# Attention keys gathered straight into key order, instead of block gathers followed by copies in SBUF

## The reference, cut to what matters

```
H, G, HD = (8, 4, 32)        # 8 query heads, 4 key/value groups, 32 channels
BLOCK = 16                   # tokens in a cache block
WINDOW = 128                 # a token attends to the 128 keys before it
SCALE = 256.0 ** (-0.5)
NBLK = 257                   # table entries of a batch
k_blocks, v_blocks: (B * NBLK, G, BLOCK, HD)
```

## Time and profile before

| | us |
|---|---|
| three timed runs | 1230.33, 1234.93, 1240.94 (median 1234.93) |
| the profiled execution | 1232.31, of which the span from first to last instruction is 1230.5 |

### The profile page before, as it was taken

One profiled execution on the slowest core, in us unless ns is written; L12 is line 12 of the kernel. 1 busy time (PEld: TensorE's weight loads), 2 busy tenths in 40 slices (PEclk: granted clock), 3 DMA queues, 4 the chain that ended last, 5 costly groups with the idle time before them and its releaser, 6 DMA issues.

```text
span 1230.5 us, 18499 instructions
## 1 busy us (share of the span) xinstructions
PE 957.4 (78%) x5487; PEld 722.4 (59%) x5487; DVE 577.4 (47%) x1672; ACT 371.8 (30%) x1034; POOL 345.6 (28%) x385
## 2 busy tenths in 40 slices
PE   3899889406999983982397878969787688999985
PEld 2677667205777763652275766657544466777774
DVE  5567766122666540584272744628323244444323
ACT  2334234102333320112171634627232223222210
POOL 7000532552555551033412221310003420343100
PEclk9899899757999996985596887969787599999999
DMA  8042207294444427632776554430211120332221
GB/s 321 5 164 42 71 31 270 94 254 135 135 133 132 135 68 170 231 115 59 151 170 110 109 107 94 93 57 0 94 47 39 65 92 9 93 96 86 77 85 52
DMA packets 71577, 132.04 MB, mean 107 GB/s; under 512 B 19841, under 2 KB 54106, under 8 KB 69168
## 3 DMA queue, kind: packets, MB, share of 16 engines
q1 hardware_dynamic: 48399, 75.49, 21.1%
q0 software_dynamic: 20800, 53.52, 16.7%
q10 hardware_dynamic: 2304, 2.13, 0.6%
HBM read 87.39 MB, written 43.30 MB: 106 GB/s over the span
## 4 chain that ended last, share of the span: by engine, by line
PE 29%; DMA 11%; issue 4%; DVE 4%; POOL 3%; ACT 3%; DVEq 0%; POOLq 0%; ACTq 0%
PE ps L436 8%; DMA early<-newblk,new_i 6%; PE ps L648 4%; DMA big<-newblk,new_i 4%; PE ps L666 3%; PE ps L1967 2%; PE ps L2110 1%; PE ps L2066 1%; PE ps L2033 1%; POOL sent_d L732 1%; PE ps L2038 1%; POOL early L970 1%; PE ps L1990 1%; POOL big L970 1%; PE ps L2067 1%
## 5 line engine op out<-in xcount | busy, mean ns | idle before, releaser
L732 POOL DMA_INDIRECT sent_d<-mid,slot_i x96 | 98.0, 1021 | 175.1 <-DVE mid L567 148.3
L723 POOL DMA_INDIRECT back_d<-early,mid x95 | 93.6, 986 | 96.3 <-DVE early L707 61.4
L694 DVE TENSOR_TENSOR early<-early,ps 128x96 f32<-128x96 f32 (+1 forms) x134 | 37.3, 279 | 141.8 <-ACT early L682 98.0
L666 PE MATMUL ps<-early 96*128 (+1 forms) x346 | 98.7, 385 | 0.9 <-DVE early L701 0.9
L677 ACT ACTIVATE early<-ps 128x256 f32<-128x256 f32 x134 | 51.4, 384 | 136.2 <-PE ps L638 126.5
L648 PE MATMUL ps<-big,early 128*128 x380 | 88.4, 357 | 5.0 <-ACT early L677 2.8
L467 DVE TENSOR_TENSOR hidl<-work,hidh 128x512 fp32r<-128x512 f32 (+1 forms) x56 | 38.8, 692 | 104.9 <-ACT hidh L461 98.3
L473 ACT ACTIVATE work<-ps 128x512 f32<-128x512 f32 (+1 forms) x56 | 33.4, 597 | 161.5 <-PE ps L436 141.3
L638 PE MATMUL ps<-late,mid 128*128 128x128 f32 x268 | 52.8, 279 | 30.5 <-DMA mid<-sent_d 30.5
L1967 PE MATMUL ps<-early 128*128 128x176 f32 x256 | 69.1, 376 | 4.5 <-DVE early L1592 4.1
L648 PEld LDWEIGHTS ps<-big,early 128*128 128x128 f32 x380 | 61.6, 195 | 18.7 <-issue 15.8
(11 more groups left out here) (378 smaller groups left out, 2224.7 us busy)
## 6 DMA issues: line engine op xcount, KB each, us to landing
mid<-sent_d SPq DMA_DIRECT2D x134, 130.0 KB
big<-back_d SPq DMA_DIRECT2D x16, 512.0 KB
early<-back_d SPq DMA_DIRECT2D x16, 256.0 KB, 3.3
sent_d<-big SPq DMA_DIRECT2D x26, 130.0 KB
big<-in_gate SPq DMA_DIRECT2D x1, 3072.0 KB, 11.9
big<-in_up SPq DMA_DIRECT2D x1, 3072.0 KB, 18.0
early<-early SPq DMA_DIRECT2D x32, 96.0 KB
big<-big SPq DMA_DIRECT2D x32, 96.0 KB
```

Of the source, the lines that this page charges most:

```text
L666: last = nc.tensor.matmul(ps[:, 6 + j % 2, 0:D], L.hTb[j % 2][0:f1 - f0, h * P:(h + 1) * P], L.down[0:f1 - f0, h, bass.ds(owners[j] * D, D ...
L694: nc.vector.tensor_tensor(L.hb[j % 2], L.sgb[j % 2], ps[:, 2 + j % 2, F:2 * F], ALU.mult)\
L723: nc.gpsimd.indirect_dma_start(out=back_d, out_offset=bass.IndirectOffsetOnAxis(ap=xblk[b % XRING][:, D:D + 1].bitcast(I32), axis=0), in_= ...
L732: nc.gpsimd.indirect_dma_start(out=sent_d, out_offset=bass.IndirectOffsetOnAxis(ap=L.slot_i[:, i:i + 1], axis=0), in_=L.rows[c][:, t, n, : ...
```

## The change

Everything below concerns how keys and values reach `kv2`, and what that needs.

- Cache and `newblk` are viewed as rows of two tokens (2 KB, 8 rows for a block). A batch's 176 keys are 88 such rows, and each is gathered straight to its partition: `old_keys(g)` issues 4 gathers of 88 rows (one for each batch) from the cache, `new_keys(g)` 4 from `newblk`. Partition p of a batch holds keys 2p and 2p+1. The copies of SP (line 866) and of POOL (line 970) are gone, and so are the staging windows.
- `kv2` has 8 slots (`KVRING`) instead of 4, four in `early` and four in `big`. `old_keys(g)` waits for `o_ps` of tile g - 8.
- The columns of the scores come in another order (even keys, then odd), which the constant for the mask takes up. Keys are transposed as 88 + 88 instead of 96 + 80 partitions, and ACT copies the transposed probabilities in one piece of 88x512 instead of two.
- The gathers need one index for each row of two keys: 88 for each batch. `pe_spread` makes them on PE by 8 small matmuls in layer 0 (chunk 3, m = 1) from the block numbers `blkw` and the new-block numbers that DVE's `windows_new` gives; `key_rows` turns them into integers on DVE at m = 2. PE waits for `index` ahead of the 8, and for `spread_used` at m = 3.
- In POOL's program `old_keys` 0 and 1 stand behind the writes of chunk 0, 2 and 3 behind those of chunk 1, 4 and 5 behind those of chunk 2. The memset of `Qbd` stands behind `new_keys` 0 and 1 and ahead of 2 and 3.
- `raw3`, a weight of layer 3 (640 KB), goes to `low0` and is loaded by SP between expert blocks 16 and 17 instead of behind the expert rows; layer 3's shared weights are loaded by SP when the first chunk's batches are done instead of after its first tile's.
- PE's loop over the 4 chunks is written out instead of a hardware loop.

```diff
+HB, HK, KVRING = BLOCK // 2, WK // 2, 8
...
-        kvw = [x[:, 0:ROW].rearrange("p (o n) -> p o n", o=BLOCK) for x in (early, big)]
         halves = [early[:, ROW:2 * ROW], big[:, 8448:8448 + ROW]]
-        kv2 = [x[:, j * (ROW // 2):(j + 1) * (ROW // 2)].rearrange("p (h b n) -> p h b n", h=2, b=BPT)
-               for x in halves for j in range(2)]
+        kv2 = [x[0:HK, j * (ROW // 2):(j + 1) * (ROW // 2)].rearrange("p (b o n) -> p b o n", b=BPT, o=2)
+               for x, n in ((early, 4), (big, 2), (halves[1], 2)) for j in range(n)]
...
             for b in range(NBK):
                 sp_block(sp, L1, b)
+                if b == XRING:
+                    sp.dma_start(raw3, a["raw3"]).then_inc(s["raw3"], 16)
...
-            for g in range(NT):
...
-                for q in range(BPT):
-                    sp.dma_start(kv2[t][0:6 * BLOCK, 0, q, :], kvw[half][p0 + q * WB:p0 + q * WB + 6, :, :])\
-                        .then_inc(s["into%d" % t], 16)
...
+            def old_keys(g):
                 t, c = g % TPC, g // TPC
...
+                if g >= TPC:
+                    pool.wait_ge(s["gold%d" % t], 16 * TPC + LANDED * c)
+                if g >= KVRING:
+                    pool.wait_ge(s["o_ps"], O_CREDIT + BPT * (g - KVRING + 1))
                 for q in range(BPT):
...
+                    gather(kv2[g % KVRING][:, q, :, :].rearrange("p o n -> p (o n)"), cache8,
+                           old_i[:, q * NT + g:q * NT + g + 1], s["gold%d" % t])
+
+            def new_keys(g):
+                t, c = g % TPC, g // TPC
+                pool.wait_ge(s["gold%d" % t], 16 * TPC + LANDED * (c + 1))
+                if g >= TPC:
+                    pool.wait_ge(s["gone%d" % t], landed(t) + LANDED * c)
+                for q in range(BPT):
+                    gather(kv2[g % KVRING][:, q, :, :].rearrange("p o n -> p (o n)"), newblk8,
+                           new_i[:, q * NT + g:q * NT + g + 1], s["gone%d" % t],
+                           bounds_check=SEGS * HB - 1, oob_is_err=False)
+
+            pool.wait_ge(s["spread_used"], 1)
...
                 pool.wait_ge(s["scattered"], (c + 1) * (16 * TPC))
                 if c == 0:
+                    pool.wait_ge(s["turn_ps"], NBK + 2 * TPC)
+                    old_keys(0)
+                    old_keys(1)
+                if c == 1:
                     pool.wait_ge(s["turn_ps"], NBK + NT)
-                    old_rows(2)
-                    old_rows(3)
+                    old_keys(2)
+                    old_keys(3)
+                if c == 2:
+                    old_keys(4)
+                    old_keys(5)
 
             pool.wait_ge(s["scattered"], 16 * NT)
-            for g in range(TPC):
-                new_rows(g)
+            for g in range(2):
+                new_keys(g)
             pool.wait_ge(s["qkv_end"], 1)
             nc.gpsimd.memset(Qbd, 0.0).then_inc(s["qzero"], 1)
+            for g in range(2, TPC):
+                new_keys(g)
             pool.wait_ge(s["qsb_ready"], NCH)
-            pool.wait_ge(s["fint_sb"], 2)
-            for g in range(TPC):
-                turn_rows(g)
-            for g in range(TPC, NT + 2):
+            for g in range(TPC + 2, NT + 2):
                 if g < NT:
...
+                    old_keys(g)
+                new_keys(g - 2)
...
-                nc.scalar.activation(PTs[0:96, n % 2, 0, :], ps[0:96, 4 + n % 2, 0:256], ACT.Copy)
-                nc.scalar.activation(PTs[0:80, n % 2, 1, :], ps[0:80, 4 + n % 2, 256:512], ACT.Copy)\
+                nc.scalar.activation(PTs[0:HK, n % 2, :, :].rearrange("p h n -> p (h n)"), ps[0:HK, 4 + n % 2, :], ACT.Copy)\
...
+            def key_rows():
+                dve.wait_ge(s["spread_ps"], 1)
+                n = BPT * NT
+                for j, idx in enumerate((old_i, new_i)):
+                    last = nc.vector.tensor_scalar(idx[:, :], ps[0:HK, 5, j * n:(j + 1) * n], float(HB),
+                                                   F["pairoff"][0:HK, :], ALU.mult, ALU.add)
+                last.then_inc(s["spread_used"], 1)
...
+            def pe_spread():
+                pe.wait_ge(s["index"], AT_SHIFT)
+                pe.wait_ge(s["slots_ready"], NCH - 2)
+                WR = BPT * WB
+                for j, x in enumerate((blkw, ix[:, 32:48])):
+                    for q in range(BPT):
+                        o = (j * BPT + q) * NT
+                        last = nc.tensor.matmul(ps[0:HK, 5, o:o + NT], F["spread"][0:WR, q * HK:(q + 1) * HK],
+                                                x[0:WR, :], start=True, stop=True)
+                last.then_inc(s["spread_ps"], 1)
...
+                    if tc == 3 and m == 1:
+                        pe_spread()
+                    if tc == 3 and m == 3:
+                        pe.wait_ge(s["spread_used"], 1)
...
                 if q == 0:
...
-                nc.tensor.transpose(ps[:, n % 2, 0:96], kv2[t][0:96, 0, q, 0:KW], ident[0:96, 0:96])
-                nc.tensor.transpose(ps[:, n % 2, 96:WK], kv2[t][0:80, 1, q, 0:KW], ident[0:80, 0:80])\
+                    pe.wait_ge(s["gone%d" % t], landed(t) + LANDED * (tc + 1))
+                nc.tensor.transpose(ps[:, n % 2, 0:HK], rows[:, q, 0, 0:KW], ident[0:HK, 0:HK])
+                nc.tensor.transpose(ps[:, n % 2, HK:WK], rows[:, q, 1, 0:KW], ident[0:HK, 0:HK])\
```

More of the change, by code:

```diff
@@ L749, in build @@
         L1.into0, L1.gone0 = [0] * AHEAD, [0] * ORING
-        L3.into0 = [loaded(j) + NCH * TURNED for j in range(AHEAD)]
-        L3.gone0 = [landed(j) + NCH * NEWROWS for j in range(ORING)]
+        L3.into0 = [loaded(j) for j in range(AHEAD)]
+        L3.gone0 = [landed(j) + NCH * LANDED for j in range(ORING)]
         gu3 = a["gu3"].rearrange("p (g k n) -> p g k n", g=2, k=KD)
@@ L1487, in _ @@
                     if tc == 3 and m == 2:
+                        key_rows()
                         token_rows()
```

84 lines of the change are left out of this document (25 added, 59 removed).

## The result

The changed kernel takes **1292.4 us** (median of four, 1288.1 to 1300.3) where the kernel before took 1234.3 beside it: a ratio of **1.047, 95% interval 1.040 to 1.054**. Forecast were 1231.4 us and "the same". The profiled execution took 1288.1 us, its span is 1286.3 (before 1230.5), the mean granted clock 0.849 (before 0.867).

The account below looks back on a forecast made before the run. PE, busy 78% of the span, was read as one chain with gaps; +0.4 - 8.2 + 4.3 = -3.5 us took the profiled 1232.3 to 1228.8, and 2.6 for the median gave 1231.4 us; range 1223 to 1246.

Parts of the forecast that it names:

- the same: Whole kernel: the change stays within 1% of the kernel before; chance 0.70.
- At nothing: Parts costed at zero: raw3's load, ACT's one copy less, the written-out loop, transposes of 88 + 88, fewer SP transfers.
- No wait there: Attention loop, later tiles: POOL's 8 gathers per tile, 10.4 us, keep ahead of PE, so no wait.
- three rivals: Slower POOL, 1245.2, chance 0.20; transfers held more than counted, 1225.4, chance 0.13; small gathers not overlapping, 1270, chance 0.05.
- the third: Rival, gathers ahead of the memset: POOL paced by each landing, 2.5 us a gather, +38 us, 1270; chance 0.05.
- Term 1: Start of the attention loop: gathers ahead of the memset take the removed copies' 10 us; +0.4 us, bounds -1.9 to +7.3.
- Term 3: Layer 0, chunk 3: making indices on PE costs a 2.2 us wait plus 2.1 us of matmuls; +4.3 us.
- first rival: Gathers ahead of the memset: each takes 1.42 us, the loop starts later; together +10.3 us, 1245.2; chance 0.20.
- Term 2: Attention chunk 0: the second tile's wait and its clock fall go, 36.8 us instead of 45.0; -8.2 us.
- the upper bound: Index making on PE in layer 0: 6.1 us if the wait also costs the clock, 1.8 us lost.
- the wait at m = 3 costs nothing: Layer 0, chunk 3: DVE's two small steps are covered by a gate and a down piece of PE; 0 us.
- The rule that spoke against it: Gathers beside DVE's work: VectorE's two-port modes block GpSimd's descriptors, so most of the 24 cache gathers would be late.

Follow-up runs that it names:

- e5: The kernel before, unaltered and profiled, beside the unaltered changed kernel; the kernel before took 1238.3 us in this batch.
- e1: The kernel before with PE's attention loop written out instead of a hardware loop; 0.998 of the kernel before, which took 1199.9 us there.
- e13: The kernel before with 16 useless gathers of 44 rows of 64 B added on POOL early in chunk 3; ratio 1.015 to the kernel before.
- e12: As e11, with old_rows(0) and old_rows(1) moved behind the writes of chunk 0; 1237.1 us, ratio 1.000 to the kernel before.
- e11: The kernel before with POOL's copies (turn_rows) issued by SP behind SP's own; 1252.3 us, ratio 1.012 to the kernel before.
- e15: The changed kernel, unaltered, run a third time, with no late update; ratio 0.989 to the kernel before.
- e14: The kernel before with only old_rows(0) and old_rows(1) moved behind the writes of chunk 0; 1188.9 us against 1202.0, ratio 0.990.
- e4: The changed kernel, unaltered, run again beside the kernel before (1238.3 us); 1297.0 us, ratio 1.047.
- e9: The changed kernel with all 128 gathers replaced by plain transfers of the same size from fixed rows, issued by SP; ratio 0.968 to the kernel before.
- e7: The changed kernel with one gather of new keys per tile instead of four, 80 gathers instead of 128; ratio 1.014 to the kernel before.
- e8: The changed kernel with the same gathers of 88 rows, but 256 B a row instead of 2 KB; ratio 1.052 to the kernel before.

## Why the prediction was wrong

**The step that failed** is in "At nothing" and in "No wait there": that POOL's gathers in the loop cost PE nothing as long as the data is in time. The data was in time, as I said: after the first tile no wait for keys is in the list. But I costed a gather only by POOL's own time and by its transfer, never by what its issuing does to PE: its matmuls are held, and its signals with them. None of the three rivals had it; the third (1270) was large enough, but by another mechanism: the pitch is 1.28 to 1.31 us for the cache and 1.36 to 1.40 for `newblk`, gathers do overlap. Chunk 0 and chunk 1 cost 38.7 and 24.5 us more.

Could the rows have told? In part. In the loop of before, where gathers come in pairs, no update of PE was over 1.8 us late. But the earlier trace rows has 26.4 us of work in 27.6 with 8 instructions of POOL beside it; the change put 47 there, and I took the ratio to be harmless. And the idle times in layer 1, where POOL scatters, were read as dependences, with 107 late updates in them; between a held and a free trace of the kernel before's work (e5 and e1) the way from the first block to the projections is 218.1 against 189.4 us. The Trainium skill (Perfetto Trace Analysis, section Tensor Engine Instruction (MATMUL, LD_WEIGHTS)) says that a matmul's end in a profile is an estimate, and that its semaphore update goes out only when PSUM has acknowledged all bytes. That agrees: the rows of e13 show PE done at 846.84 and ACT released at 861.45. It doesn't say what holds the update.

**Term 1, the start (+0.4)**: right in its working, off by its starting point. From POOL's first write to the first scores it was 74.3 us before (and 522.24 for the write), forecast 74.7, measured 76.8:

```profile
514.54 0.98 POOL L969 DMA_INDIRECT newblk<-early,tok_i  x1 [45.85 <-DVE early L1573]
...
578.20 1.09 POOL L896 DMA_INDIRECT early<-newblk,new_i  x1 [2.36 <-DMA newblk<-big,tok_i]
...
587.83 1.07 POOL L896 DMA_INDIRECT early<-newblk,new_i  x1 [0.30 <-issue]
588.90 0.97 POOL L990 MEMSET early<- 128x1024 f32 x1
```

The memset came at 588.9 instead of 599.0 (594.7 and term 3), the scores at 591.3 and released by DVE's query copies, as said. The last landed write cost 2.36 us, the lower bound, not 4.6. Four of 24 cache gathers took 1.37 to 1.66 us, and five of the 16 writes 1.4 to 2.5, where DVE works. That is the first rival's mechanism, but at a third of its gathers or less, so it decided nothing. The miss is that the first write came 7.7 us earlier: the wait of 21.4 us for combination rows ends at 481.6, and my list of waits began at 500, so it was not in the argument at all. It fell by 11.9 us (e12 against e11 shows why).

**Term 2 (-8.2)**: right when free. The second tile's wait is gone in every trace of the changed kernel, and chunk 0's scores to tail take 35.1 us in e15 (564.9 to 600.0; forecast 36 to 38). Against e14, which is free too and has the old copies, that is 6.2 us less (41.3). When held it was buried.

**Term 3 (+4.3)**: right mechanism, size off. Chunk 3 of layer 0, from 175.5 to the last matmul at 219.0 before, 177.0 to 227.2 now: 50.2 instead of 43.5, so +6.7. Free it was 46.6 (e15) against 43.0 (e14), +3.6. PE's wait was 1.8 us, the matmuls 1.9; the rest is the clock, 0.50 behind them in the profiled run of after, 1.00 in that of e15:

```profile
187.88 0.80 PE L1823 MATMUL ps<-blkw,big 44*88 44x16 f32 x8 [1.77 <-issue]
...
189.70:195.00 5.30, 5.30 (x13) 4.15 (x14) 0.71 (x2) 0.00 (x0) 4.05 (x5) 0.50 0.61 232
```
```profile
188.50:194.00 5.50, 5.50 (x26) 4.41 (x25) 2.25 (x6) 1.23 (x2) 4.28 (x5) 1.00 0.61 225
```

13 records in 5.3 us where the other has 26 in 5.5: 2.6 us, the loss that I had put at 1.8 and into the upper bound only. The update that ends these matmuls was 3.4 us late as well, with POOL's sends of tokens beside it; "the wait at m = 3 costs nothing" was off by the 0.4 us that PE waited there.

**The ledger of the spans** (1230.5 to 1286.3, by the same points of both traces): layer 0 +8.2 (6.7 of it in chunk 3); from there to the first projection -15.9, of which 11.9 are the combination wait; to the first scores +2.5; chunk 0 +38.7; to chunk 1's scores +1.5; chunk 1 +24.5; the rest -3.7. Sum +55.8. The other 4.0 us between layer 0 and the projections don't come back in the second held pair: there, from e5 to e4, this part fell by 11.5 us and the wait in it by 12.6. `raw3`, the transposes of 88 + 88, ACT's one copy and SP's fewer transfers show nowhere as a loss; chunks 2 and 3 are 1.2 to 2.5 us shorter than before, when no gather runs beside them.

**The rule that spoke against it** in the prediction (the Trainium skill, SBUF — State Buffer, section SBUF: two separate sides: VectorE's two-port modes keep GpSimd from writing descriptors) fits the few stretched rows above, 9 of 40. What decided was an effect the other way round, from GpSimd's issuing to TensorE.

**What stays open**: why a batch is held or free. One chip was free in one batch (before 1199.9) and held in a later one (1229.6), so it isn't the chip alone; the traces don't tell which of its cores ran. Nor is shown what in POOL's issuing does it, nor whether PE is slow because its signals can't leave or the other way round. The Trainium skill (DMA: Bandwidth & Descriptors, section SWDGE vs HWDGE vs iDMA) says that GpSimd writes its descriptors into rings in SBUF, and that transfers issued by SyncE or ScalarE don't take this path. e9 agrees with the second half, at 0 late updates in the attention; that the rings are the place where TensorE is held no run here shows. The only free number for the unaltered changed kernel against before is 0.989, the only held ones 1.047 and 1.047.

## What to carry to other kernels

Count how many indirect transfers an engine issues back to back beside a chain that passes from TensorE to another engine and back, not only their bytes: here each gather in such a burst cost 0.9 to 1.3 us of the chain when held (63.2 us for the 71 instructions of POOL in chunks 0 and 1, 20.8 for 16 in e13), while the same bytes issued by SyncE cost nothing. Few large gathers, gathers beside stretches in which the critical engine hands over seldom, or plain transfers from another queue keep out of the way; pacing shortens each hold far more than the sum. And a large gather should not start beside a load that the critical engine waits for. Where TensorE shows gaps from "issue" and its consumers waits from "remote", compare the end of the producing matmul with the start of its consumer, counting both by batch, since the matmul that ended last may belong to the next one. And count late updates in a part that the change leaves alone, to know under which condition a trace was taken, before believing either sign.

## What the runs showed of the hardware

- Under one of two conditions TensorE is held while GpSimd issues indirect DMAs closely: its matmuls start with gaps, and its semaphore updates come late, by up to 1.9 us behind a pair of gathers (e5), 4.3 behind bursts of five (e7), 8.6 behind bursts of eight (e4) and 18.6 behind one of 24 (e4). DVE's signals to ACT in the same loop took 0.04 us. Row size (64 B in e13, 256 B in e8, 2 KB) and the load of the transfer engines (0.01 to 0.28) make no difference.
- The updates held longest in e4 come 1.3 to 2.7 us after the last gather of a burst of eight or 24, in e13 3.6 us after it.
- Under the other condition none was late by more than 0.31 us in the attention, with 28 gathers in 36 us (e15), and none over 0.3 us in layer 1, where it is 100 to 109 under the first. The kernel before differs by 27 to 38 us (2 to 3%) between the two conditions, and the sign of this change with it: 1.047 or 0.989.
- Plain transfers of GpSimd (four in 2.5 us, e5) made no update late by themselves; every late one of e5's loop has a gather within the 5 us before it.
- A gap of 1.8 us in front of matmuls with 16 columns and the 1.9 us of those matmuls stood ahead of a granted clock of 0.50 over the next 5.3 us in the changed kernel's first trace; in e15, with a gap of 1.9 us at the same place, the clock stayed at 1.00.
- An indirect DMA occupied GpSimd for 0.97 to 1.09 us whether it had 88 rows of 2 KB or 128 of 1 KB, one every 1.28 to 1.40 us; 9 of 40 beside DVE's work took 1.4 to 2.5.
